# Where VectorE makes the one-hots in a graph kernel's edge loop

## The reference

```
q = (X @ Wq)[src];  k = (X @ Wk)[dst];  e = tanh(q + k)
scores = e @ Wphi;  scores = scores - max(scores)
denom = segment_sum(exp(scores), src);  alpha = exp(scores) / (denom[src] + 1e-9)
msg = alpha * ((X @ Wy_w + Wy_b)[dst] + e @ We)
out = layernorm(X + segment_sum(msg, src))
```

## Time and profile before

| | us |
|---|---|
| median of 3 runs | 5739.93 |
| lowest, highest | 5734.63, 5740.55 |
| span of the profiled execution | 6222.6 |
| VectorE busy in it | 4448.3 (71%) |
| TensorE busy in it | 3737.4 (60%) |
| GpSimd busy in it | 3607.5 (58%) |
| ScalarE busy in it | 2763.2 (44%) |

### The profile page before, as it was taken

The page is one execution under the profiler, slowest core; times in us unless marked ns, Lnnn a source line. Parts: engine busy times, 40 slices in busy tenths (PEclk is TensorE's granted clock), DMA queues, the critical chain, the costliest instruction groups (busy, mean ns, idle before and its releaser), DMA issues. The chain is left out here.

```text
span 6222.6 us, 88097 instructions
## 1 busy us (share of the span) xinstructions
PE 3737.4 (60%) x19333; PEld 2790.7 (45%) x19333; DVE 4448.3 (71%) x9850; ACT 2763.2 (44%) x10900; POOL 3607.5 (58%) x3540
## 2 busy tenths in 40 slices
PE   7799999945555545544554555554455555555556
PEld 6555555534444444444444444444344444444445
DVE  7688888866666676666766667666667666677666
ACT  3688888833333333333333333333333333333336
POOL 1032333346666666666666666666666666667661
PEclk9766666666666677667777666667666666677678
DMA  2200000023333333333333333333333333333334
GB/s 78 64 4 4 4 4 4 5 65 92 92 89 92 92 92 90 92 89 92 92 93 89 93 89 94 90 93 92 90 91 92 89 92 89 92 92 93 92 89 102
DMA packets 283763, 477.87 MB, mean 77 GB/s; under 512 B 94209, under 2 KB 203363, under 8 KB 282984
## 3 DMA queue, kind: packets, MB, share of 16 engines
q0 software_dynamic: 165184, 324.30, 20.0%
q1 hardware_dynamic: 100262, 142.95, 6.9%
q10 hardware_dynamic: 17794, 4.91, 0.4%
HBM read 456.43 MB, written 20.60 MB: 77 GB/s over the span
## 5 line engine op out<-in xcount | busy, mean ns | idle before, releaser
L1086 POOL DMA_INDIRECT gathered<-table,dst_rows x3276 | 3267.9, 998 | 1538.2 <-issue 936.2
L1120 PE MATMUL bank<-gathered,weighted_onehots 128*128 128x193 f32 x6592 | 1952.2, 462 | 1107.1 <-DVE block_sums L1196 682.1
L1120 PEld LDWEIGHTS bank<-gathered,weighted_onehots 128*128 128x128 f32 x6592 | 1640.0, 276 | 1274.1 <-issue 1090.8
L1196 DVE TENSOR_TENSOR block_sums<-block_sums,bank 128x193 f32 x3296 | 1170.1, 355 | 1060.8 <-remote 526.6
L1129 ACT ACTIVATE gathered<-gathered 128x256 f32<-128x256 f32 x824 | 347.6, 422 | 2797.9 <-DVE gathered L1173 1808.2
L1109 PE MATMUL bank<-q_parts,src_onehots_T 128*128 x3296 | 628.3, 330 | 1253.7 <-DVE src_onehots_T L1154 616.5
L1169 DVE TENSOR_REDUCE gathered<-bank 128x128 f32<-128x384 f32 x1648 | 838.7, 551 | 369.2 <-DMA gathered<-table,dst_rows 169.2
L1140 ACT ACTIVATE weighted_onehots<-src_onehots,edge_weight 128x128 f32<-128x128 bf16 x3296 | 1076.9, 398 | 27.1
L1109 PEld LDWEIGHTS bank<-q_parts,src_onehots_T 128*128 128x128 bf16 x3296 | 400.1, 122 | 1501.4 <-issue 1457.4
L817 ACT ACTIVATE places_past_far<-bank,stat 128x98 bf16<-128x98 f32 x2727 | 891.2, 399 | 126.6 <-issue 53.8
L859 POOL DMA_INDIRECT sorted_list<-sorted_groups,unit_destinations x248 | 318.5, 1284 | 814.0 <-DVE sorted_groups L787 750.1
(11 more groups left out here) (183 smaller groups left out, 2185.6 us busy)
## 6 DMA issues: line engine op xcount, KB each, us to landing
src_in_block_rows<-src_in_block_list SPq DMA_DIRECT2D x206, 512.0 KB
gathered<-table,dst_rows POOLq DMA_INDIRECT x3276
gathered<-table SPq DMA_DIRECT2D x2560, 0.8 KB
table<-in_x SPq DMA_DIRECT2D x4, 1562.5 KB
x_in<-in_x SPq DMA_DIRECT2D x24, 256.0 KB, 2.9
x_again<-in_x SPq DMA_DIRECT2D x48, 128.0 KB, 2.3
out<-out_rows SPq DMA_DIRECT2D x48, 128.0 KB, 1.9
sorted_list<-sorted_groups,unit_destinations POOLq DMA_INDIRECT x248
```

The source lines that it names most:

```text
L1086: e.indirect_dma_start(slot[:, r, j, 0:ROW], None, table, bass.IndirectOffsetOnAxis(ap=gidx[:, t:t + 1].bitcast(u32), axis=0)).then_inc(ga ...
L1120: made = e.matmul(SM[q % 2 * 2 + j // 2][:, o:o + SUMS], ohw[:, q % 3, j, :], slot[:, r, j, A:SLOT], start=True, stop=True)
L1196: e.tensor_tensor(sums[:, bass.ds(b, SUMS)], sums[:, bass.ds(b, SUMS)], SM[q % 2 * 2 + j // 2][:, o:o + SUMS], ALU.add).then_inc(accumulat ...
```

## The change

In `vector_steps` both kinds of one-hots of a chunk were made at its first step, ahead of everything else in that step. Now the first step of each part of the pass makes both at its start; after that, the transposed one-hots of the next chunk are made in the second step of the present chunk, and the plain ones in the fourth, each behind the scores (L1182) and ahead of the sums (L1196) of that step. The waits are the same and written for the chunk that is made. No other engine's code changes.

```
+        def turned_onehots(e, c):
+            e.wait_ge(lows_loaded[c % LOB], 16 * (c // LOB + 1))
+            if c >= 2:
+                e.wait_ge(queried, (c - 1) * QUADS_PER_CHUNK)
+            e.tensor_scalar(ohT[:, c % 2, :], lob[:, c % LOB, :], part0[:, :], None, ALU.is_equal).then_inc(onehots_T_made, 1)
+
+        def onehots(e, c):
+            if c >= 2:
+                e.wait_ge(weighted, (c - 1) * QUADS_PER_CHUNK)
+            e.tensor_tensor(oh[:, c % 2, :, :, :], lo[:, c * CHUNK:(c + 1) * CHUNK].rearrange("p (q a j) -> p q a j", a=1, j=QUAD)
+                            .to_broadcast([PARTS, QUADS_PER_CHUNK, PARTS, QUAD]),
+                            row1c[:, :, :].rearrange("p (a n) j -> p a n j", a=1).to_broadcast([PARTS, QUADS_PER_CHUNK, PARTS, QUAD]),
+                            ALU.is_equal).then_inc(onehots_made, 1)
+
         def vector_steps(e, regs, first, end, limit):
...
             for step in range(first, end):
-                q = step
-                if q < limit and q % QUADS_PER_CHUNK == 0:
-                    c = q // QUADS_PER_CHUNK
...
+                if step == first and step < limit:
+                    turned_onehots(e, step // QUADS_PER_CHUNK)
+                    onehots(e, step // QUADS_PER_CHUNK)
                 if step < 3:
...
                     e.tensor_reduce(score[:, q * QUAD:(q + 1) * QUAD], ephi[:, k], AX.X, ALU.add).then_inc(scored, 1)
+                q = step
+                c = q // QUADS_PER_CHUNK + 1
+                if q < limit and c * QUADS_PER_CHUNK < limit:
+                    if q % QUADS_PER_CHUNK == 1:
+                        turned_onehots(e, c)
+                    elif q % QUADS_PER_CHUNK == 3:
+                        onehots(e, c)
                 q = step - 4
                 if 0 <= q < limit:
```

## The result

| | median us | range |
|---|---|---|
| before | 5740.55 | 5734.63 to 5743.27, 5 runs |
| after | 5724.91 | 5716.85 to 5729.06, 5 runs |

The ratio is 0.9965, 95% interval 0.9951 to 0.9979. Timed again later beside 17 runs of before, it was 0.9972 (0.9962 to 0.9983). So the change saves about 16 us; the forecast was 60 us more.

A forecast was written before the change was run, and what follows sets the result against it. GpSimd's gather issue was taken as the bound, with one-hots holding gathers up: 206 x (1.20 - 0.91) = +60 us, other terms nought, so 5739.9 + 60 = 5800 us; range 5640 to 5860, 8 in 10.

The forecast's parts named there:

- The kernel is bound by GpSimd's gather issue: Edge loop: 3276 gathers at 1.252 us take at least 4102 us; the rest is extra GpSimd time per chunk.
- the "remote" stalls: GpSimd's 509.3 us of ring waits in the first profile, taken as belonging to the profiled execution and left out.
- The port's price before, 0.91 us a chunk: Edge loop before: 188 us left over, read as one-hots on VectorE holding up GpSimd's gathers.
- the 4102 + 13.4: Edge loop: 4102 us of gather pitch plus 13.4 us of first ring wait while the pipeline fills.
- TensorE freed of its wait, nought: TensorE's 616.5 us of idle for L1154 at chunks' first steps goes; gain nought, at most 92.7 us.
- L1196 later, waits and row loads, nought: L1196 0.66 and 1.14 us later, nought; buffer waits free; row loads 0, at most 15 us at four places.
- The start within the pitch, after the change: Moved one-hots start 0.08 us ahead of a gather and cost 1.57 us a chunk, taken as 1.20; +60 us.
- the 1.02 worked out: Forecast cost in us of L1157 after the change, started 0.08 us ahead of a gather, by the 0.83 us rule.
- the first rival: Other side of the edge: one-hots start just inside a gather, 0.1 to 0.4 a chunk; -115 us, 5625; chance 0.17.
- the 1.20 of the forecast: Port price in us a chunk taken after the change, against 0.91 before.
- the 0.35 of that rival: Port price a chunk used for the other side of the edge: 206 x (0.35 - 0.91) = -115 us.
- The Trainium skill's rule: Port lock of VectorE and GpSimd: first half accepted, second not; taken whole it would be the rival of no change.

The follow-up runs named there:

- n1: Kernel before with both one-hots cut to a few elements from the third chunk on, so its sums are not the reference's: 5570.43 us, ratio 0.9714.
- the account: Table setting the spans of eleven profiled executions against n1's span plus what their gathers are busy more than in n1; no timed run of its own.
- the second profile: The kernel before, unchanged, profiled again: 5741.02 us, ratio 0.9999.
- w1: Changed kernel plus a wait of VectorE for its own scores of that step ahead of each moved one-hot: 5630.48 us, ratio 0.9819.
- w2: Kernel before plus a wait of VectorE for its own last sum ahead of the transposed one-hots: 5612.33 us, ratio 0.9795.

## Why the prediction was wrong

- *The kernel is bound by GpSimd's gather issue.* Right, and shown by n1 and the account. That the "remote" stalls belong to the profiled execution was wrong in its reason: under that condition the runs that are not profiled take 6251 to 6302 us too. In the ordinary condition the profile adds nothing (5726.46 us for the profiled run of after, 5716.85 to 5729.06 for the others). The conclusion, to take them out, held: the loop was put at 4303 us and has 4293 in the second profile.
- *The port's price before, 0.91 us a chunk.* Measured 0.80 over n1. The rest was in the remainder that I had divided by 206: n1's loop takes 4131.7 us, 16 more than the 4102 + 13.4 that I took for its floor, and the loop of before 10 less than 4303.
- *TensorE freed of its wait, nought.* Right: no ring waits before or after; the idle time (733.2 us in the second profile, at every chunk and not at every other) was worth nothing.
- *L1196 later, waits and row loads, nought.* Right as far as waits go: VectorE waited 4.3 us in all for the source numbers of L1147. But SyncE's load of them (512 KB a chunk, L1061) moved with the transposed one-hots, and that had an effect that I hadn't looked for; it is in the next point.
- *The start within the pitch, after the change.* This step failed. "2.71 + 2.22 - 4 x 1.252 = -0.08" took one landing time for all steps. Here is the changed kernel: GpSimd's last gather of a step and the first of the next, SyncE's load of the source numbers, and VectorE's step that waits for the rows:

```profile
3500.77 0.95 POOL L1086 DMA_INDIRECT gathered<-table,dst_rows  x1 [0.31 <-issue]
3502.03 0.95 POOL L1086 DMA_INDIRECT gathered<-table,dst_rows  x1 [0.30 <-PE bank L1120]
...
3501.52 0.35 SPq L1061 DMA_DIRECT2D src_in_block_rows<-src_in_block_list  x1
...
3504.46 1.02 DVE L1173 TENSOR_REDUCE gathered<-bank 128x128 f32<-128x384 f32 x2 [1.24 <-DMA gathered<-table,dst_rows]
...
3508.66 1.02 DVE L1173 TENSOR_REDUCE gathered<-bank 128x128 f32<-128x384 f32 x2 [0.21 <-DMA gathered<-table,dst_rows]
```

  3504.46 - 3500.77 = 3.69 us, not 2.71; the next step's rows were taken 2.9 us after their last gather's start. The load stands 0.75 us behind the last gather of the step. It is issued when L1147 is done, so the change brought it there: of the 206 steps that are gathered just then, 118 have a last gather of usual length and VectorE waiting for the rows, and their median is 3.68 us. The same steps in the second profile of before have 2.72 us, with the load issued 1.5 to 2 us into the gathers of the step before them. Even there, 14 waited-for steps have the load close to their last gather, and they have a median of 3.85 us. No run moves the load alone, so that it delays the rows is read from the two traces and not tested. VectorE was also often late by itself: a step in which the changed kernel makes transposed one-hots began with a wait for rows 52 times of 206 (159 in the second profile of before), one in which it makes plain ones 119 times (195 before), so the landing didn't set the start in the others.

  Counted over the trace, 87 of the 206 plain one-hots started up to 0.15 us ahead of a gather's start, as forecast (75 of them by 0.05 to 0.15 us, at 1.0 us each), the others somewhere inside a pitch; of the transposed 64. The mean was 0.77 to 0.79 us a chunk and not 1.20. The price of each start was right (1.93 us for one of 1.22 across the start: 0.98 against the 1.02 worked out); their share was mis-sized. The edge that the first rival named was the real lever: w1 crossed it with 0.12 us and is 101 us below before in its batch; the rival had given 115. The 16 us that the change gained were in no term: the price after it came out between the 1.20 of the forecast and the 0.35 of that rival, since the starts were spread over both sides of the edge.
- *The size of the gain.* 0.80 to 0.77 or 0.79 is 2 to 6 us between single profiles; the times say 14 to 16. The other 10 us are of the size by which one kernel's profiles differ, and I can't place them.
- *The Trainium skill's rule* (SBUF — State Buffer, "SBUF: two separate sides"), that whoever starts first holds the shared port pair for its whole instruction: the gather of 1.93 us agrees for VectorE as the first. For GpSimd as the first it holds only for a part: in w2 L1156, 0.53 us into a gather, is stretched by 0.19 us where the gather had 0.41 us to go, and in w1 L1152, 0.02 us into one, runs in 1.23 us where 0.93 us were to go. That the hold-up is that port pair was not tested by itself.

## What to carry to other kernels

Where GpSimd's DMA issue sets the pace, ask of each long VectorE instruction when it starts within GpSimd's pitch, not only how long it is: here a shift of 0.12 us was worth 1.5 to 2%, and moving the same instruction to another step 0.3%. The ones seen to hold up a gather here (L756, L1154, L1157) have 16-bit operands and take 0.75 us and more; in n1, where beside two short one-hots only float32 ones of up to 0.56 us are left, the gathers keep their median of 0.947 us. Whether type or length decides was not tested. A one-line wait for the engine's own last result is a cheap way to try it. And compare a profile's span with the times first: when they differ by 8%, as 6222.6 and 5739.9 did, profile again before reading phases of tenths of a microsecond out of it.

## What the runs showed of the hardware that I had not expected

In the eleven profiles of the account, each of the 323 gathers that starts 0.03 to 0.16 us after a plain one-hot's start takes 1.88 to 2.01 us. Each of the 421 that start less than 0.03 us after it or up to 0.1 us ahead of it takes 0.94 to 0.97. The last cheap one starts 0.027 us after the one-hot, the first dear one 0.030: a cliff, 1 us high, and the self-wait's 0.12 us crossed it. And in the edge loop TensorE's semaphore increments were late by microseconds in the profiles of three batches and in the first profile, with spans of 6223 to 6304 us, whatever the kernel.
